# Channel mix: the shifted tokens in rows of 512 columns, their last 128 tokens in a tile of their own

## The reference, cut to what matters

```python
xc = _ln(_ln(x2, ln2_g, ln2_b), cm_g, cm_b)   # (2048, 512)
xcs = _shift(xc)                              # row t holds token t-1, row 0 is zero
kc = jnp.square(jax.nn.relu(xcs @ Wck))       # Wck 512 x 2048
vc = kc @ Wcv                                 # Wcv 2048 x 512
rc = jax.nn.sigmoid(xc @ Wcr)                 # Wcr 512 x 512
return x2 + rc * vc
```

## Time and profile before

| | |
|---|---|
| median of 3 runs | 1049.67 us (1048.85 to 1050.69) |
| the profiled execution | 1056.41 us, its span 1054.7 us |
| PE busy | 1035.4 us, 98% of the span |
| DVE, ACT, POOL busy | 62%, 52%, 41% |
| mean DMA rate | 185 GB/s |
| share of PE in the chain that ended last | 91% |

### The profile page before, as it was taken

The page is one execution under the profiler, slowest core; times in us unless marked ns, Lnnn a source line. Parts: engine busy times, 40 slices in busy tenths (PEclk is TensorE's granted clock), DMA queues, the critical chain, the costliest instruction groups (busy, mean ns, idle before and its releaser), DMA issues.

```text
span 1054.7 us, 18034 instructions
## 1 busy us (share of the span) xinstructions
PE 1035.4 (98%) x5378; PEld 852.3 (81%) x5378; DVE 656.1 (62%) x1188; ACT 551.7 (52%) x944; POOL 428.4 (41%) x332
## 2 busy tenths in 40 slices
PE   6999999999999999999999999989999999999998
PEld 2556888888788878887887888879999999999986
DVE  7967948904590458041008398947777777777746
ACT  5963546333433343333345443347777777777742
POOL 1021304221222122202223423367778888888532
PEclk9999999999999999999999999989999999999999
DMA  9905296516421643334264891066988989988688
GB/s 291 384 9 196 90 346 207 176 60 241 160 99 60 239 159 99 99 120 160 100 213 154 292 298 71 1 214 129 260 193 254 237 193 323 218 163 167 93 283 343
DMA packets 102389, 195.05 MB, mean 185 GB/s; under 512 B 15544, under 2 KB 39096, under 8 KB 101824
## 3 DMA queue, kind: packets, MB, share of 16 engines
q1 hardware_dynamic: 82944, 158.70, 43.3%
q0 software_dynamic: 18816, 34.64, 17.3%
q10 hardware_dynamic: 576, 1.05, 0.4%
HBM read 141.98 MB, written 63.18 MB: 195 GB/s over the span
## 4 chain that ended last, share of the span: by engine, by line
PE 91%; DVE 4%; issue 2%; ACT 1%; DMA 1%; POOL 1%; POOLq 0%; ACTq 0%; DVEq 0%
PE bank L683 42%; PE bank L1018 23%; PE bank L1637 14%; PE bank L588 5%; PE bank L1627 3%; DMA tdb<-in_L_attn_time_decay 1%; PE bank L1029 1%; PE bank L1039 1%; PE bank L1089 1%; POOL mix_lo L395 0%; DVE bns L257 0%; DVE hb L854 0%; PE bank L642 0%; PE bank L625 0%; DVE mx L384 0%
## 5 line engine op out<-in xcount | busy, mean ns | idle before, releaser
L995 POOL TENSOR_TENSOR ksp_lo<-ra,ksp_hi 128x512 fp32r<-128x512 f32 x94 | 140.3, 1492 | 435.6 <-ACT ksp_hi L938 435.4
L1637 PEld LDWEIGHTS bank<-xT,wus 128*128 128x128 f32 x1344 | 163.8, 192 | 7.2
L1637 PE MATMUL bank<-xT,wus 128*128 128x128 f32 x1344 | 164.3, 276 | 0.0
L1018 PE MATMUL bank<-vring,ksp_hi 128*128 128x512 f32 x512 | 159.4, 393 | 0.0
L930 ACT ACTIVATE ra<-bank 128x512 f32<-128x512 f32 x96 | 57.4, 598 | 173.8 <-PE bank L683 169.5
L1789 DVE TENSOR_TENSOR wd_lo<-w,wd_hi 128x1024 fp32r<-128x1024 f32 x84 | 103.0, 1226 | 49.0 <-ACT wd_hi L1717 30.8
L683 PE MATMUL bank<-wd_hi,aT 128*128 128x512 f32 x336 | 126.8, 418 | 4.0 <-DVE aT L1783 4.0
L938 ACT ACTIVATE ksp_hi<-ra 128x512 fp32r<-128x512 f32 x96 | 60.7, 632 | 120.0 <-PE bank L1018 119.5
L1018 PEld LDWEIGHTS bank<-vring,ksp_hi 128*128 128x128 f32 x512 | 95.5, 188 | 20.0
L683 PE MATMUL bank<-xcT_hi,wck_lo 128*128 128x512 f32 x256 | 101.7, 397 | 0.0
L683 PE MATMUL bank<-xcT_lo,wck_hi 128*128 128x512 f32 x256 | 101.5, 396 | 0.0
(11 more groups left out here) (293 smaller groups left out, 2081.6 us busy)
## 6 DMA issues: line engine op xcount, KB each, us to landing
vring<-wcv_d SPq DMA_DIRECT2D x64, 512.0 KB, 3.3
w<-in_L_ffn_Wu SPq DMA_DIRECT2D x32, 512.0 KB
w<-in_L_ffn_Wd SPq DMA_DIRECT2D x32, 512.0 KB
hT_d<-hT SPq DMA_DIRECT2D x16, 512.0 KB, 3.9
hTb<-hT_d SPq DMA_DIRECT2D x3, 2048.0 KB
raw_wcv<-in_L_attn_Wcv SPq DMA_DIRECT2D x4, 1024.0 KB, 6.9
raw_wck<-in_L_attn_Wck SPq DMA_DIRECT2D x4, 1024.0 KB, 9.6
add_d<-zrow SPq DMA_DIRECT2D x1, 4096.0 KB, 20.4
```

The source lines that it names most:

```text
L995: nc.gpsimd.tensor_tensor(ksp[1][:, i % 2], ra[:, i % 2], ksp[0][:, i % 2], ALU.subtract).then_inc(sem("klo_in"), 1)
L1018: m = nc.tensor.matmul(bank[to + j][:], ksp[l][:, i % 2, j * P:(j + 1) * P], rhs(r), start=i == 0 and k == 0, stop=i == last and k == 2)
L1637: m = nc.tensor.matmul(bank[4 + u][:, n * P:(n + 1) * P], wus[u][:, c * EI + n * P:c * EI + (n + 1) * P], xT4[:, u, c * P:(c + 1) * P], st ...
```

## The change

The tile of the shifted tokens gets rows of exactly 512 columns, 2048 bytes, with hi and lo in one tile. Column 0 is the token before the block, and columns 1 to 511 are the block's first 511 tokens. Token 512 no longer has a place there. The block's last 128 tokens, which the fourth receptance tile needs, are written a second time into a tile of their own, `xc3`, of 128 columns per chunk, at 186 KB. The last column of `xc3` is copied by DVE into a small tile `carry`, from which ACT fills column 0 of the next block.

```diff
-        xcT = [at(f"xcT_{s}", [P, C, BLK + 1], R, 136 + 8.0625 * n) for n, s in enumerate(("hi", "lo"))]
+        xcT_t = at("xcT", [P, 2, C, BLK], R, 136)
+        xcT = [xcT_t[:, s] for s in range(2)]
+        xc3 = at("xc3", [P, 2, C, P], R, 186)
+        carry = at("carry", [P, 2, C], R, 152.0625)
...
             wait_apart(dve, sem("x2_in"), 32 if isinstance(b, int) else 16 * b + 16)
+            if isinstance(b, int) and b:
+                dve.wait_ge(sem("rcp_in"), BT)
...
         def dve_lo_xc(dve, b, first=False):
             for c in range(C):
-                dve.wait_ge(sem("hiT_in"), b * C + c + 1)
-                nc.vector.tensor_tensor(xcT[1][:, c, 1:BLK + 1], bank[TURNED[-1][c] if first else 6 + c % 2][:], xcT[0][:, c, 1:BLK + 1],
+                rows = bank[TURNED[-1][c] if first else 6 + c % 2]
+                dve.wait_ge(sem("hiT_in"), 2 * (b * C + c + 1))
+                nc.vector.tensor_tensor(xcT[1][:, c, 1:], rows[:, 0:BLK - 1], xcT[0][:, c, 1:],
                                         ALU.subtract).then_inc(sem("loT_in"), 1)
+                nc.vector.tensor_tensor(xc3[:, 1, c], rows[:, BLK - P:], xc3[:, 0, c],
+                                        ALU.subtract).then_inc(sem("loT_in"), 1)
+            wait_apart(dve, sem("loT_in"), 2 * (b * C + C))
+            nc.vector.tensor_copy(carry[:], xc3[:, :, :, P - 1]).then_inc(sem("carry2"), 1)
...
-            for s in range(2):
-                nc.vector.memset(xcT[s][:, :, 0:1].bitcast(F), 0.0).then_inc(sem("carry2"), 1)
+            nc.vector.memset(xcT_t[:, :, :, 0].bitcast(F), 0.0).then_inc(sem("carry2"), 1)
...
             act.wait_ge(sem("trT_in"), b * C + 1)
             if first:
-                act.wait_ge(sem("carry2"), 2)
+                act.wait_ge(sem("carry2"), 1)
             else:
-                for s in range(2):
-                    nc.scalar.activation(xcT[s][:, :, 0:1], xcT[s][:, :, BLK:BLK + 1], ACT.Copy).then_inc(sem("carry2"), 1)
-                act.wait_ge(sem("carry2"), 2 + 2 * b)
+                act.wait_ge(sem("carry2"), 2 * b)
+                nc.scalar.activation(xcT_t[:, :, :, 0], carry[:], ACT.Copy).then_inc(sem("carry2"), 1)
+                act.wait_ge(sem("carry2"), 2 * b + 1)
             for c in range(C):
                 act.wait_ge(sem("trT_in"), b * C + c + 1)
-                nc.scalar.activation(xcT[0][:, c, 1:BLK + 1], bank[TURNED[-1][c] if first else 6 + c % 2][:], ACT.Copy).then_inc(sem("hiT_in"), 1)
+                rows = bank[TURNED[-1][c] if first else 6 + c % 2]
+                nc.scalar.activation(xcT[0][:, c, 1:], rows[:, 0:BLK - 1], ACT.Copy).then_inc(sem("hiT_in"), 1)
+                nc.scalar.activation(xc3[:, 0, c], rows[:, BLK - P:], ACT.Copy).then_inc(sem("hiT_in"), 1)
...
             if c >= 2 and not opening:
-                pe.wait_ge(sem("loT_in"), b * C + c - 1)
+                pe.wait_ge(sem("loT_in"), 2 * (b * C + c - 1))
...
         def pe_block2(pe, b, first=False, last=False):
-            pe.wait_ge(sem("loT_in"), b * C + C)
+            pe.wait_ge(sem("loT_in"), 2 * (b * C + C))
...
-                split_product(bank[6 + j % 2][:], lambda s, c: xcT[s][:, c, 1 + j * P:1 + (j + 1) * P],
+                split_product(bank[6 + j % 2][:], lambda s, c: xc3[:, s, c] if j == BT - 1 else xcT[s][:, c, 1 + j * P:1 + (j + 1) * P],
                               lambda s, c: wcr[s][:, c], C).then_inc(sem("rcp_in"), 1)
...
-                pe_inner_up(pe, b * NCI + i, i % 4, [m[i // 4] for m in wck], lambda s, c: xcT[s][:, c, 0:BLK])
+                pe_inner_up(pe, b * NCI + i, i % 4, [m[i // 4] for m in wck], lambda s, c: xcT[s][:, c])
```

## The result

The changed kernel takes 1045.29 us (median of 5 runs, 1043.50 to 1046.18), beside 1049.91 us for the kernel before in the same comparison: a ratio of 0.9953, 95% interval 0.9941 to 0.9966. In a later comparison, in which the kernel before took 1054.05 us, the ratio was 0.9944 (0.9926 to 0.9962). The forecast was 1043.5 us, a ratio of 0.9941: the gain came out at 4.6 us where 6.15 were worked out.

The account below looks back on a forecast made before the run. TensorE (PE) was taken to bound the kernel, busy 1035.4 of 1054.7 us. The terms 6.4 + 0.3 - 0.55 = 6.15 us took the 1049.67 us median to 1043.5 us, range 1042.2 to 1047.2 us.

Parts of the forecast that it names:

- Up groups, 6.4 us: Stage 2, 12 matmuls streaming xcT against Wck: would run at stage 3's pace, gaining 6.4 us over four blocks.
- Receptance product, 0.3 us: Stage 2, 48 matmuls with xcT as weights: only the fourth tile, now xc3, speeds up, gaining 0.3 us in four blocks.
- Short pieces, 0.55 us: Opening of stage 2: PE waits for the added 128-column copies and subtractions, then starts slower, losing 0.55 us.
- The later boundaries and the carry: Three later block boundaries in stage 2: added pieces and the copied last column hide behind down groups, cost 0.
- Does the gain last?: Behind stage 2: later work starts from PE events and moves forward together, so the whole 6.15 us stays.
- The tile isn't the cause: Stage 2: whatever slows xcT's products stays, so nothing is gained and the time is 1050.2 us; chance 0.07.
- only the ragged ends cost: Stage 2 streams: misaligned rows cost at most four columns, 1.0 us in 64 groups; time 1049.2 us, chance 0.04.
- half: Stage 2: only 3.5 us gained from faster groups, time 1046.7 us; chance 0.13 together with costly 128-column pieces.
- dear short pieces: Block openings: 128-column pieces cost as whole ones, 2.2 + 1.2 us, time 1046.4 us; chance 0.13 shared with a halved gain.
- The phases coincide: Stage 2: xcT, Wck and Wcr at the same place in 2048-byte rows, reads meet, slower, 1055.6 us; chance 0.06.

Follow-up runs that it names:

- late pieces: Changed kernel, but in the first block DVE makes its four 128-column pieces after the four of 511, awaited only before the fourth receptance tile: 1043.79 us, ratio 0.9941.

## Why the prediction was right, and where it was not

The forecast of 1043.5 us and the measured 1045.29 us are 1.8 us apart. By the traces up to the end of stage 3 the terms 6.4 + 0.3 - 0.55 came out as some 5.8, 0.2 and -0.65, and behind stage 2 another 0.3 us was won.

*Up groups, 6.4 us.* The size was close, the reason was wrong. From the first up group to the end of the last down group stage 2 took 406.08 us (149.60 to 555.68) before and 400.12 us (150.51 to 550.63) after: 5.96 us. Of these the three receptance products in it gave 0.15. The term was 0.6 us too large, for the most part because it applied the steady difference of a pair, 0.1025 us, to all 14 pairs of a block, while some of them hold transposes and logits of the router and start slowly in both layouts: the up group behind the first logits took 237.9 ns a matmul before (from 376.24 us) and 236.3 ns after (from 373.75 us), averaged over its starts.

The step that failed is the naming of the trait. The prediction put the excess down to the tile's pitch of 2052 bytes and to starts 4, 8 or 12 bytes off a multiple of 16. Rows at multiples of 64 bytes (2112, 64 bytes off) were as slow as before, and rows at 60 modulo 64 were faster. What counts, as far as the runs go, is the place of a tile against the others modulo 256 bytes: 0 and 256 give 38.08 us for seven pairs, 60 gives 38.26, 64 gives 38.73, 128 gives 38.69, and moving all tiles together by 64 changes nothing. The kernel with a pitch of 2112 bytes has both cases in one group: its chunk 0, at a multiple of 256, ran at 0.227 us a matmul, the other chunks at 0.236. The forecast held because hTb, which it copied the pace from, agreed with the new xcT in this property too. That much was luck: the same change with xcT 64 or 128 bytes further on satisfies the trait that the prediction named and gains 0.08 or 0.16%, both within the noise or next to it.

*Receptance product, 0.3 us.* Tile 3 went from 2.80 to 2.76 us (its first matmuls still follow slow ones), tiles 0 to 2 from 8.38 to 8.36, the whole product from 11.17 to 11.12: 0.05 us a block, 0.2 us in all. The prediction left open whether pitch or start mattered; the answer is the place of the weights, counted here from that of the streamed rows: 4, 64 and 68 bytes off are slow, 0 and 132 are at full pace.

*Short pieces, 0.55 us.* Measured 0.65 us, by the mechanism that was stated: PE begins 0.57 us late instead of 0.44, and the product that begins behind the pause loses some 0.1 us, as worked out. The step of 0.20 us and the finish of DVE (2.4 + 0.88 us after its start) came out too. What the sum left out is that DVE starts later: 2.91 us before PE was due in the kernel before (135.52 and 138.43), and 2.80 us in the changed one (135.94 and 138.74). Its wait now counts two pieces of ACT instead of one. The later boundaries and the carry cost nothing, as expected, with 0.5 us to spare instead of 0.65, since DVE starts 0.17 us later behind ACT there.

*Does the gain last?* Up to the end of stage 3: 6.0 - 0.6 is 5.4, and 5.64 us arrived. PE waits 0.9 us longer for hTb (1.4 against 0.5), and a wait of 0.9 us for DVE's tail is gone. Behind stage 3 it stays open. The two ratios, 0.9953 and 0.9944 with their intervals, leave anything from 4 to 6 us possible. From the start of the last matmul on hTb to the end of the span the kernels with rows of 2112 and 2064 bytes, which have the pace of before, take 359.5 and 360.1 us, the changed kernel 360.8 and, a second time, 362.6, and the one with late pieces 360.1: one or two us may come back there, but two traces of one kernel differ by as much.

*The rivals.* "The tile isn't the cause", "only the ragged ends cost" and "half" are refuted by up groups of 2.72 us with down groups of 2.72 us behind them, and dear short pieces by their step of 0.20 us. The Trainium skill's rule of 16-byte cachelines (SBUF — State Buffer, Specifications (TRN2)) doesn't account for the loss here: at a pitch of 2064 bytes every row began at a multiple of 16, and seven pairs took 38.78 us as before. "The phases coincide" had the wrong sign: coinciding phases are the fast case. But its object, the place of a stream against the weights, was the right one, and it came nearer to the cause than the forecast did.

*What the receptance product adds.* Its streams (Wcr) stay where they are in all these runs, and only its weights move with xcT. Tiles 0 to 2 take 8.36 us with the weights 4 bytes off, 8.40 at 64 and 8.16 at 132. So the place of xcT counts where it is only loaded as weights, with nothing changed among the streams; and the nine slow matmuls in a group with xcT 64 bytes off show that differing neighbours aren't needed.

*What stays open.* Why 132 bytes are harmless for weights while 128 bytes are harmful for a stream, and whether a stream meets the weights of its own matmul or those of the next. Every run moved xcT against all other tiles at once, so that its partner is PE's other operand, and not a tile that another engine uses, is argued and not shown. A meeting of two reads is an argument for it, not shown. Moving Wcr and xc3 so that the receptance product runs at full pace beside fast up groups would be worth up to 0.97 us, the sum of what its 191 recorded matmuls take over 0.2267 us; it was not tried.

## What to carry to other kernels

When one product runs some per cent slower than others of its shape and nothing waits, compare where its tiles begin modulo 256 bytes against the tiles that it meets, and move it; starts at multiples of 16 or 64 bytes didn't help by themselves. A control that agrees with the changed kernel in several properties gives the size of a gain and not its cause, and one changed number in a declaration is enough to tell them apart. Before the spans of two profiles are subtracted, look for a stretch with a lower granted clock in one of them.

## What the runs showed of the hardware that had not been expected

- A matmul of 512 columns follows the last one after 0.2267 us, or, averaged over an up group, after 0.228 to 0.234 us, by the place of one of its operands, xcT, against the other tiles modulo 256 bytes, with no wait in the profile. Over a kernel with 768 such matmuls and as many behind them it was 0.5% of the time.
- The loss doesn't grow with the offset: streams 60 bytes off cost about three tenths of what 64 or 128 bytes off cost ((38.26 - 38.08) against 0.65 and 0.61 us).
- The groups behind a slow one are slow at first, though their own tiles are well placed; with xcT 64 bytes off, a pair's 0.09 us of loss fell on up and down groups about equally (230.1 and 230.5 ns a matmul, averaged over the starts in stage 2). With xcT 128 bytes off most of it fell on the up groups (2.79 us, and 2.74 us for a down group).
